# A transformer block on one Trainium2 core: where the users of one shared PSUM bank stand in the first token group

## The chip, the cores and the metric

The kernel runs on one core of one Trainium2 chip. The metric is device time in microseconds (us), lower is better. A core has TensorE for matrix products (PE in the profile, PEld its weight loads), VectorE (DVE), ScalarE (ACT), GpSimd (POOL) and SyncE (SP, which here issues the transfers). The engines run side by side and wait for each other only through semaphores.

## The reference: what is computed

```python
xn = _layernorm(x, axis=-1)                    # x: 2 x 2048 tokens of 1024 channels
s = _L0_attn_ref(xn)                           # autocorrelation of a token, best 6 lags, softmax, shifted sum
g = _silu(_L0_ffn_ref(xn, w1q, a1, b1, w3q, a3, b3, w2q, a2, b2))
x = x + s * g
...
def _qlora_linear(x, wq, A, B):
    w = jnp.tile(wq, (1, 4))
    return x @ w.T + (x @ A.T @ B.T) * 0.5
gate = jax.nn.silu(_qlora_linear(x, w1q, a1, b1))      # hidden size 2752, rank 2
up = _qlora_linear(x, w3q, a3, b3)
return _qlora_linear(gate * up, w2q, a2, b2)
```

Since a weight is tiled four times, the four quarters of a token are summed first and multiplied by one quarter of the weight. If lag zero of the autocorrelation beats all others by a wide margin, the softmax gives it all the weight and `s` is `xn`; the kernel shows that margin with a small transform and keeps a general path for tokens where it fails.

## The kernel before: groups, chunks and the bank mb

The 4096 tokens are 8 groups of 512 (`i` from 0 to 7), a group 4 tiles of 128 (`q`). The hidden size is walked in 22 chunks, called pairs in the code (`p` from 0 to 21). For a pair TensorE forms the gate product in a bank `g` and the up product in a bank `u` (`up`, lines 1305 to 1327), six matmuls each, since every float32 operand is split in a high and a low fp16 part. The rank-2 terms come from `lora` (L1300), which runs ahead of each odd pair and serves that pair and the even one before it. ScalarE applies silu (`gate`), VectorE multiplies (`product`, writes `h`), and `z2` (L1412) and the down products follow. A bank `g`/`u` of pair p is free again when `product` of pair p-3 is done.

The order on every engine is written out by hand: small tables (`X_AT`, `C_AT`, `I_AT`, `HIGH_AT`, `LOW_AT`, `NORM_AT` and so on) say after which pair each piece of side work stands. Engines run their lists in order, so an instruction that waits holds all that is behind it on its engine.

In group 0 the kernel has side work that later groups don't have. It prepares the weights: a bound of each block's size (`w_bound`, squares with a sum, output `w_sq`), the power-of-two scale (`w_scale`), the high part on ScalarE (`w_high`, outputs `w_h`, `wp_h`) and the low part on VectorE (`w_low`, outputs `w_l`, `wp_l`). It forms the rank-4 projection of its own tokens (`z0`, `z0_spread`), split in three bf16 parts: `z_part[0]` and `z_part[1]` on ScalarE, `z_rest` and the last part with `zst` on VectorE. And it transposes the tokens of group 1 on TensorE (`second_x`, L1370, eight half tiles, each copied out by ScalarE to `xT`).

One PSUM bank, `mb`, is shared by all of this in turn: the eight half tiles of `second_x`, two `odd_power` products (L1337, each squared by ScalarE in `square`, output `sq`), the product `lags` (L1347), reduced by VectorE in `lag_gap` (L834, output `gp`, semaphore `gap_done`), and the one-column `flag_sum`. A user may write only when the one before it has been read.

GpSimd makes the quarter sums of the next group's tokens, `sums(i + 1, q)`: outputs `yh`, `xq`, `dd`, each a tensor_tensor on SBUF, as soon as ScalarE's `normalise` has written `xn` for that tile.

The waits in `second_x` before the change, with half tiles numbered `n` from 0 to 7:

```python
if n == 2:
    pe.wait_ge(wall_read, 3)
elif n == 4:
    pe.wait_ge(sq_done, 2)
elif n == 6:
    pe.wait_ge(gap_done, 1)
```

Of the kernel before, what the change touches and what calls it, by code (L numbers as in the profile page):

```python
# [16 lines left out]
NG = TOK // G  # L17
# [77 lines left out]
def build(nc, d):  # L95
# [3 lines left out]
    with ExitStack() as ctx:  # L99
# [9 lines left out]
        def sem(name):  # L109
            return ctx.enter_context(nc.semaphore(name))  # L110
# [95 lines left out]
        def block_cols(b):  # L206
            return pair_col(BLOCK[b]), HID if b == NB - 1 else pair_col(BLOCK[b + 1])
# [61 lines left out]
        x1_ready, x1_done = sem("x1_ready"), sem("x1_done")  # L269
# [15 lines left out]
        c_ready, sq_done, i_ready, gap_done = sem("c_ready"), sem("sq_done"), sem("i_ready"), sem("gap_done")  # L285
# [22 lines left out]
        STATS_AT = [(3, 7, 10, 14)] + [(1, 7, 13, 19)] * (NG - 1)  # L308
        NORM_AT = [(5, 10, 13, 17)] + [(2, 8, 14, 20)] * (NG - 1)
        Z_AT = [{}] + [{3 + 6 * q + r: (q, r) for q in range(3) for r in range(4)}] * (NG - 1)  # L310
        X_AT = {3: (0, 0), 4: (0, 1), 6: (1, 0), 7: (1, 1), 12: (2, 0), 13: (2, 1), 16: (3, 0), 17: (3, 1)}
        W2L_AT = {16: 0, 18: 1}
        C_AT = [(9, 11)] + [(5, 9)] * (NG - 1)
        I_AT = [(14,)] + [(11,)] * (NG - 1)
        FAR_AT = [(8, 12, 16, 20)] + [(4, 10, 16)] * (NG - 1)
        FAR0_AT = (5, 6, 7, 9)
        FLAG_AT = [18] + [18] * (NG - 1)
# [228 lines left out]
        def _(act):  # L546
            def A(out, in_, f=ACT.Identity, **kw):
                return nc.scalar.activation(out, in_, f, **kw)  # L548
# [25 lines left out]
            def gate(i, p):  # L574
                n = pair_rows(p)
                act.wait_ge(g_ready, at_pair(i, p))
                if p >= 2:
                    act.wait_ge(mult_done, at_pair(i, p - 2))
                A(sil[0:n, p % 2, :], gb[p % 3][0:n, :], ACT.Silu, scale=winv[0:n, 3 * block_of(p):3 * block_of(p) + 1]).then_inc(sil_done, 1)
# [30 lines left out]
            def second_x(n):  # L610
                q, half = n // 2, n % 2
                act.wait_ge(x1_ready, n + 1)
                A(xT1[:, 4 * half:4 * half + 4, q * P:(q + 1) * P],
                  mb[:].rearrange("p (k t) -> p k t", k=4), ACT.Copy).then_inc(x1_done, 1)
# [23 lines left out]
            def w_bound(b, m):  # L638
                lo, hi = block_cols(b)
                act.wait_ge(w_loaded[b][m], 16)  # L640
                if b or m:
                    act.wait_ge(wsum_done, 2 * b + m)
                with nc.allow_low_precision(reason="a bound with a margin"):
                    A(w_sq[:, :, 0:hi - lo], raw_w[b][:, m], ACT.Square,
                      accum_out=wsum[:, 2 * b + m:2 * b + m + 1]).then_inc(wsum_done, 1)

            def w_high(b, m, k=0):
                lo, hi = block_cols(b)
                s = wscl[:, 3 * b + m:3 * b + m + 1]
                act.wait_ge(wscl_done, min(b, 2) + 1)  # L650
                if b == 0:
                    A(wt_h[m][:, k, lo:hi], raw_w[b][:, m, k, :], scale=s).then_inc(wh_done, 1)
                    return
                if b == NB - 1:
                    A(wp_h[:, :, 64 * m:64 * m + 64], raw_w[b][:, m, :, hi - lo - 64:hi - lo], scale=s)
                A(wt_h[m][:, :, lo:min(hi, LAST * P)], raw_w[b][:, m, :, 0:min(hi, LAST * P) - lo],
                  scale=s).then_inc(wh_done, 1)
# [9 lines left out]
            def b_scale(b):  # L667
                lo, hi = BLOCK[b] // 2, BLOCK[b + 1] // 2
                act.wait_ge(b_rest_done, 2 if b < 2 else 4)
                act.wait_ge(wscl_done, min(b, 2) + 1)  # L670
                s = wscl[:, 3 * b + 2:3 * b + 3]
                if b == NB - 1:
                    hi = LAST // 2
                    A(bst[0:64, hi, :], bst[0:64, hi, :], ACT.Copy, scale=s[0:64])
                    A(bst[64:96, hi, 0:64], bst[64:96, hi, 0:64], ACT.Copy, scale=s[64:96])
                    A(bst[64:96, hi, 64:P], bst[64:96, hi, 64:P], ACT.Copy, scale=half_u[64:96, 0:1])
                A(bst[:, lo:hi, :], bst[:, lo:hi, :], ACT.Copy, scale=s).then_inc(b_done, 1)
# [45 lines left out]
            A(rsb[:], mb[:], ACT.Copy).then_inc(rsb_done, 1)  # L723
            w_high(0, 1, 1)
            w_bound(1, 0)
            act.wait_ge(z0_ready, 2)
            A(z_part[0][:], mb[:], ACT.Copy).then_inc(z0_part, 1)
            w_bound(1, 1)
            act.wait_ge(z0_rest, 1)
            A(z_part[1][:], z_rest[:], ACT.Copy).then_inc(z0_part, 1)  # L730
            b_scale(0)
            for i in range(NG):
                last = i + 1 == NG
                for p in range(NP_):
                    gate(i, p)
                    if i == 0:
                        if p in X_AT:
                            second_x(2 * X_AT[p][0] + X_AT[p][1])
                        for b, m in HIGH_AT.get(p, ()):
                            w_high(b, m)  # L740
                        if p in B_AT:
                            b_scale(B_AT[p])
                        for b, m in BOUND_AT.get(p, ()):
                            w_bound(b, m)
                        if p in CAST_AT:
                            b_cast(CAST_AT[p])
                        if p in W2_AT:
                            w2_high(W2_AT[p])
                    if p in C_AT[i]:
                        square(i, C_AT[i].index(p))  # L750
                    if i == 0 and p in FAR0_AT:
                        far_lags(0, FAR0_AT.index(p))
                    if not last and p in NORM_AT[i]:
                        normalise(i + 1, NORM_AT[i].index(p))
                    if not last and p in FAR_AT[i]:
                        far_lags(i + 1, FAR_AT[i].index(p))
                    if p % 4 == 1 and p > 1:
                        folded_high(i, p // 4 - 1)
                    if i == 0 and p == LAST:
                        b2_high()  # L760
                tail_shifts(i)
                folded_high(i, HN)
                if i and not last:
                    far_lags(i + 1, 3)
                z2_copies(i)
                if i == 0:
                    second_z()
                for q in range(4):
                    if i and not last and q == 3:
                        z_copy(i + 1)  # L770
                    down(i, q)
                    if i == 0 and q:
                        first_mean(q - 1)
                if i == 0:
                    first_mean(3)
# [3 lines left out]
        def _(dve):  # L779
# [379 lines left out]
            for i in range(NG):  # L1159
# [4 lines left out]
                for p in range(NP_):  # L1164
                    if i == 0 and p - 1 in I_AT[0]:
                        lag_gap(0)
# [14 lines left out]
                    if i == 0 and p == 4:  # L1181
                        w_scale(2, 2, mb[:, 0:6])
                    if i and p - 1 in I_AT[i]:
                        lag_gap(i)
# [49 lines left out]
        def _(pe):  # L1234
# [103 lines left out]
                o.then_inc(c_ready, 1)  # L1338

            def lags(i):  # L1340
                if i == 0:
                    pe.wait_ge(x1_done, 6)
                pe.wait_ge(sq_done, at_group(i, 2, 2))
                for q in range(4):
                    t = slice(q * P, (q + 1) * P)
                    for c in range(2):
                        o = mm(mb[:, t], sq[:, c, t], inv[:, 0, :], start=c == 0, stop=c == 1)  # L1347
                o.then_inc(i_ready, 1)
# [5 lines left out]
            def second_x(q, half):  # L1354
                n = 2 * q + half
                buf, loaded, count = front_buf(1, q)
                pe.wait_ge(loaded, count)
                if n == 0:
                    pe.wait_ge(z0_rest, 1)
                else:  # L1360
                    pe.wait_ge(x1_done, n)
                if n == 2:
                    pe.wait_ge(wall_read, 3)
                elif n == 4:
                    pe.wait_ge(sq_done, 2)
                elif n == 6:
                    pe.wait_ge(gap_done, 1)
                for k in range(4):
                    c = P * (4 * half + k)
                    o = nc.tensor.transpose(mb[:, k * P:(k + 1) * P], buf[:, c:c + P], ident[:])  # L1370
                o.then_inc(x1_ready, 1)
# [177 lines left out]
            for i in range(NG):  # L1549
# [3 lines left out]
                for p in range(NP_):  # L1553
# [3 lines left out]
                    if i == 0 and p == 5:  # L1557
                        pe.wait_ge(x1_done, 2)
                        scale_sum(2, mb, 0)
                        scale_sum(3, mb, 3)  # L1560
                    if i == 0 and p in X_AT:
                        second_x(*X_AT[p])
                    if p in C_AT[i]:
                        odd_power(i, C_AT[i].index(p))
                    if p in I_AT[i]:
                        lags(i)
# [83 lines left out]
```

## Time and profile before

| | |
|---|---|
| time, median of 3 runs | 848.99 us (848.12 to 849.02) |
| the profiled execution | 848.62 us, its span 846.8 us |
| PE busy | 830.9 us, 98% of the span |
| DVE / ACT / POOL busy | 577.6 / 331.2 / 148.0 us (68 / 39 / 17%) |

The span is the stretch between the first and the last instruction that the profiler records; the 1.8 us around it belong to the execution's own time. A line of the timeline gives the start, the duration, the engine, the source line, the operation, what it writes and reads, and in brackets the idle time of the engine before it with the instruction that ended it. Durations of neighbours overlap a little, since instructions are pipelined; the pitch from one start to the next is the time that an instruction takes of its engine. All times of the timeline are from the span's start. Matmul ends are modelled.

### The profile page before, as it was taken

The page shows a single profiled execution, that of the slowest core. Times are in us where ns is not written, and L with a number is a line of the kernel's source. Part 1 is how long each engine was busy: PE and PEld are TensorE (multiplying, and loading weights), DVE is VectorE, ACT ScalarE, POOL GpSimd, SP SyncE. Part 2 cuts the span into 40 slices and gives each one's busy share as a digit, 9 for nine tenths or more (in the row PEclk, how much of TensorE's full clock was granted, in tenths as well). Part 3 has the DMA queues.
Part 4 walks back from the last instruction along what each step waited for, and adds up shares of the span by engine and source line. Part 5 has one row for each costly group of instructions (what it writes and reads, how often), then busy time and mean ns, then how long its engine had stood idle before and what let it go on. Part 6 is the DMA issues. An engine that isn't in the chain of part 4 may idle for free.

```text
span 846.8 us, 11242 instructions
## 1 busy us (share of the span) xinstructions
PE 830.9 (98%) x4200; PEld 441.2 (52%) x4200; DVE 577.6 (68%) x941; ACT 331.2 (39%) x544; POOL 148.0 (17%) x240
## 2 busy tenths in 40 slices
PE   6998999999999999999999999999999999999997
PEld 4443575335744367334763347534575336844366
DVE  7888744686776876688667776678766686744535
ACT  5886645434133342333423333333323434122231
POOL 5224101222012220122201221023201222000000
PEclk9999999999999999999999999999999999999999
DMA  9721026000230003300042000501015000220004
GB/s 285 269 89 50 26 107 218 26 26 26 82 142 26 26 26 125 100 26 26 26 151 74 26 26 26 199 28 48 26 49 176 26 1 0 101 100 1 1 2 149
DMA packets 18903, 62.13 MB, mean 73 GB/s; under 512 B 2464, under 2 KB 4224, under 8 KB 18576
## 3 DMA queue, kind: packets, MB, share of 16 engines
q1 hardware_dynamic: 18832, 61.28, 21.1%
q8 instruction: 33, 0.54, 0.3%
q14 instruction: 38, 0.31, 0.1%
HBM read 44.49 MB, written 16.78 MB: 72 GB/s over the span
## 4 chain that ended last, share of the span: by engine, by line
PE 87%; DVE 5%; ACT 3%; issue 2%; DVEq 2%; DMA 1%; SPq 0%; POOL 0%; ACTq 0%; POOLq 0%
PE g L1249 25%; PE u L1249 23%; PE zb L1412 5%; PE g L1471 4%; PE u L1471 4%; PE u L1480 4%; PE g L1480 4%; PE u L1478 4%; PE g L1478 4%; PE g L1300 3%; PE mb L1337 1%; DMA xf<-in_x 1%; DVEq L868 1%; PE g L1474 1%; PE u L1474 1%
## 5 line engine op out<-in xcount | busy, mean ns | idle before, releaser
L548 ACT ACTIVATE sil<-g,winv 128x512 f32<-128x512 f32 (+1 forms) x176 | 119.8, 683 | 267.1 <-PE g L1300 239.2
L852 DVE SCALAR_TENSOR_TENSOR h<-u,winv,sil 128x512 f32<-128x512 f32 x168 | 125.6, 749 | 122.6 <-ACT sil L548 107.1
L1249 PE MATMUL g<-xt,w_h 128*128 128x512 f16 x656 | 196.2, 381 | 0.0
L1249 PE MATMUL u<-xt,w_h 128*128 128x512 f16 x656 | 195.1, 379 | 0.0
L809 DVE CUSTOM_DVE_ANT_0 junk<-xn,abc 128x1024 bf16<-128x1024 f32 x96 | 120.3, 1253 | 6.0 <-issue 2.7
L1249 PE MATMUL u<-xt,w_l 128*128 128x512 f16 x328 | 124.3, 379 | 0.0
L1249 PE MATMUL g<-xt,w_l 128*128 128x512 f16 x328 | 124.3, 379 | 0.0
L1249 PEld LDWEIGHTS u<-xt,w_h 128*128 128x128 f16 x656 | 64.2, 98 | 77.4
L1249 PEld LDWEIGHTS g<-xt,w_h 128*128 128x128 f16 x656 | 55.6, 98 | 83.3 <-issue 31.6
L449 POOL TENSOR_TENSOR ve<-mv,three 128x1 f32<-128x1 f32 x30 | 6.5, 218 | 471.9 <-DVE mv L791 471.8
L548 ACT ACTIVATE gg<-g 128x512 f32<-128x512 f32 x32 | 19.1, 598 | 139.8 <-PE g L1474 64.1
L1003 DVE SCALAR_TENSOR_TENSOR ob<-xr,c_mean,gg 128x1024 f32<-128x1024 f32 x27 | 34.6, 1283 | 55.6 <-ACT gg L548 34.4
L1471 PE MATMUL g<-w_h,hf_h 128*128 128x512 f32 x174 | 71.8, 413 | 0.3 <-ACT gg L548 0.3
L1471 PE MATMUL u<-w_h,hf_h 128*128 128x512 f32 x174 | 69.0, 396 | 0.0
L1480 PE MATMUL u<-w_h,hf_l 128*128 128x512 f32 x145 | 57.5, 397 | 0.0
L1480 PE MATMUL g<-w_h,hf_l 128*128 128x512 f32 x145 | 57.4, 396 | 0.0
L1478 PE MATMUL u<-w_l,hf_h 128*128 128x512 f32 x145 | 57.4, 396 | 0.0
L1478 PE MATMUL g<-w_l,hf_h 128*128 128x512 f32 x145 | 57.4, 396 | 0.0
L864 DVE TENSOR_TENSOR acc<-acc,h 128x512 f32<-128x512 f32 x80 | 56.8, 710 | 0.0
L1249 PEld LDWEIGHTS g<-xt,w_l 128*128 128x128 f16 x328 | 32.1, 98 | 38.7
L1249 PEld LDWEIGHTS u<-xt,w_l 128*128 128x128 f16 x328 | 32.1, 98 | 38.7
L1412 PE MATMUL zb<-h,a2st 128*6 128x512 f32 x352 | 48.5, 593 | 0.0
(255 smaller groups left out, 1131.2 us busy)
## 6 DMA issues: line engine op xcount, KB each, us to landing
xr<-in_x SPq DMA_DIRECT2D x32, 512.0 KB, 4.6
out_x<-ob SPq DMA_DIRECT2D x31, 512.0 KB, 2.9
xf<-in_x SPq DMA_DIRECT2D x30, 512.0 KB, 3.3
raw_w<-in_w2t SPq DMA_DIRECT2D x1, 2560.0 KB
abc<-in_a SPq DMA_DIRECT2D x1, 2048.0 KB, 8.2
raw_w<-in_w1t SPq DMA_DIRECT2D x2, 768.0 KB, 8.5
raw_w<-in_w3t SPq DMA_DIRECT2D x2, 768.0 KB, 9.8
raw_w<-in_w1t SPq DMA_DIRECT2D x1, 704.0 KB, 12.8
```

The lines of the kernel that those rows point to most:

```text
L548: return nc.scalar.activation(out, in_, f, **kw)
L809: nc.vector.tensor_tensor_reduce(junk[:], xn[:], abc[:, r, :], 1.0, 0.0, ALU.mult, ALU.add, zt[:, q, r:r + 1]).then_inc(z_done, 1)
L852: stt(out=h[0:n, p % NH, :], in0=up, scalar=winv[0:n, 3 * block_of(p) + 1:3 * block_of(p) + 2], in1=sil[0:n, p % 2, :], op0=ALU.mult, op1= ...
L864: o = tt(acc[0:rows, b, :], a, h[0:rows, p % NH, :], ALU.add)
L1003: stt(out=o[:], in0=x[:], scalar=c_mean[:, q:q + 1], in1=gg[:], op0=ALU.subtract, op1=ALU.mult)
L1249: o = mm(bank[:], a, x, start=opens and t == 0, stop=closes and t == len(terms) - 1)
L1300: o = mm((gb, ub)[s % 2][k % 3][:], bst[32 * s:32 * s + 32, p // 2, :], zst[32 * s:32 * s + 32, :], start=s >= 2 and not first, stop=s < 2 ...
L1412: o = mm(zb[c:c + 6, :], a2st[:, p, :], h[:, p % NH, :], start=n == 0, stop=p + 4 >= NP_)
L1471: mm(bank[:], hf_h[:, n, t], w2_h[:, n, c:c + 512], start=n == 0, stop=False)
L1474: mm(bank[:], hf_l[:, n, t], w2_l[:, n, c:c + 512], start=False, stop=True).then_inc(dn_ready, 1)
L1478: mm(bank[:], hf_h[:, n, t], w2_l[:, n, c:c + 512], start=False, stop=False)
L1480: mm(bank[:], hf_l[:, n, t], w2_h[:, n, c:c + 512], start=False, stop=False)
```

## The change

Five edits, all in group 0 or ahead of it.

1. `X_AT`: the third tile of `second_x` (half tiles 4 and 5) moves from after pairs 12 and 13 to after pairs 14 and 15. The fourth stays after 16 and 17.
2. `I_AT[0]`: `lags` moves from after pair 14 to after pair 13, and with it `lag_gap` on VectorE, from ahead of `product(15)` to ahead of `product(14)`.
3. Waits on TensorE follow: half tile 4 now waits for `gap_done` instead of the squares, half tile 6 for no reader but ScalarE's copy of half tile 5, and `lags` no longer waits for half tile 5's copy.
4. On ScalarE in group 0 `square` stands ahead of `w_high`, `b_scale` and the other weight work of the same pair.
5. Ahead of group 0 `w_bound(1, 1)` stands before `z_part[0]` instead of behind it.

```diff
-        X_AT = {3: (0, 0), 4: (0, 1), 6: (1, 0), 7: (1, 1), 12: (2, 0), 13: (2, 1), 16: (3, 0), 17: (3, 1)}
+        X_AT = {3: (0, 0), 4: (0, 1), 6: (1, 0), 7: (1, 1), 14: (2, 0), 15: (2, 1), 16: (3, 0), 17: (3, 1)}
...
-        I_AT = [(14,)] + [(11,)] * (NG - 1)
+        I_AT = [(13,)] + [(11,)] * (NG - 1)
@@ -723,9 +723,9 @@
             w_bound(1, 0)
+            w_bound(1, 1)
             act.wait_ge(z0_ready, 2)
             A(z_part[0][:], mb[:], ACT.Copy).then_inc(z0_part, 1)
-            w_bound(1, 1)
             act.wait_ge(z0_rest, 1)
@@ -736,6 +736,8 @@
                         if p in X_AT:
                             second_x(2 * X_AT[p][0] + X_AT[p][1])
+                        if p in C_AT[0]:
+                            square(0, C_AT[0].index(p))
                         for b, m in HIGH_AT.get(p, ()):
                             w_high(b, m)
@@ -746,7 +748,7 @@
-                    if p in C_AT[i]:
+                    if i and p in C_AT[i]:
                         square(i, C_AT[i].index(p))
@@ -1338,8 +1340,6 @@
             def lags(i):
-                if i == 0:
-                    pe.wait_ge(x1_done, 6)
                 pe.wait_ge(sq_done, at_group(i, 2, 2))
@@ -1362,8 +1362,6 @@
                 if n == 2:
                     pe.wait_ge(wall_read, 3)
                 elif n == 4:
-                    pe.wait_ge(sq_done, 2)
-                elif n == 6:
                     pe.wait_ge(gap_done, 1)
```

TensorE's instructions before, from the end of pair 12 on (L1370 is `second_x`, L1300 `lora`, L1412 `z2`, L1347 `lags`, L1249 a pair's products):

```order
L1370 MATMUL mb<-ident,xf_65 128x128 [waits sq_done,x1_done,x0_loaded]
...
L1412 MATMUL zb<-h,a2st 6x512 [waits mult_done]
L1412 MATMUL zb<-h,a2st 6x512 x3
L1370 MATMUL mb<-ident,xf_65 128x128 [waits x1_done,x0_loaded]
...
L1347 MATMUL mb<-inv,sq 128x128 [waits sq_done,x1_done]
L1347 MATMUL mb<-inv,sq 128x128 x7
L1300 MATMUL g<-zst,bst 128x512 [waits mult_done]
```

And now, over the same pairs (line numbers of the changed file; L1368 is `second_x`, L1302 `lora`, L1410 `z2`, L1251 a pair's products):

```order
L1410 MATMUL zb<-h,a2st 6x512 [waits mult_done]
L1410 MATMUL zb<-h,a2st 6x512 x3
L1347 MATMUL mb<-inv,sq 128x128 [waits sq_done]
L1347 MATMUL mb<-inv,sq 128x128 x7
...
L1368 MATMUL mb<-ident,xf_65 128x128 [waits gap_done,x1_done,x0_loaded]
L1368 MATMUL mb<-ident,xf_65 128x128 x3
L1302 MATMUL g<-zst,bst 128x512 [waits mult_done]
```

The transposes after pairs 12 and 13 are gone, `lags` follows `z2` of pair 13 at once, and the first transposes after it, at the end of pair 14, carry the wait for VectorE's reduction.

VectorE's instructions before, from `w_low` of pair 12 on (L1081 and L1085 are `w_low`, L852 `product`, here of pairs 13 and 14, L864 `add_chunk`, L788 to L791 `stats`, L887 `folded_low`, L834 `lag_gap`):

```order
L1081 SCALAR_TENSOR_TENSOR wp_l<-raw_w_134,wscl,wp_h 128x64 [waits wh_done]
L1085 SCALAR_TENSOR_TENSOR w_l<-raw_w_134,wscl,w_h 128x640
L852 SCALAR_TENSOR_TENSOR h<-u,winv,sil 128x512 [waits u_ready,z2_done,sil_done] x2
L864 TENSOR_TENSOR acc<-h 128x512 [waits hfl_done,mult_done]
L788 BN_STATS bn<-xf_66 128x6 [waits stats_done,x1_loaded]
L789 BN_STATS bn<-xf_66 128x6
L791 BN_AGGR mv<-bn 128x2
L887 TENSOR_TENSOR hf_l<-acc,hf_h 128x512 [waits hfh_done]
L834 TENSOR_REDUCE gp<-mb 128x4 [waits i_ready]
```

And now (L1083 and L1087 are `w_low`, L854 `product`, L836 the reduction):

```order
L1083 SCALAR_TENSOR_TENSOR wp_l<-raw_w_134,wscl,wp_h 128x64 [waits wh_done]
L1087 SCALAR_TENSOR_TENSOR w_l<-raw_w_134,wscl,w_h 128x640
L854 SCALAR_TENSOR_TENSOR h<-u,winv,sil 128x512 [waits u_ready,z2_done,sil_done]
L836 TENSOR_REDUCE gp<-mb 128x4 [waits i_ready]
```

The reduction stands right behind `product(13)`, five instructions earlier than before, but still behind all of `w_low` of pair 12.

ScalarE's instructions before, from `gate(12)` on (sil is `gate`, xT `second_x`, dd,far `far_lags`, bst `b_scale`, w_h from raw_w_137 `w2_high`, xn `normalise`, here of group 1's third tile):

```order
L548 ACTIVATE sil<-g,winv 128x512 [waits mult_done,g_ready]
L548 ACTIVATE xT_147<-mb 128x4x128 [waits x1_ready]
L548 ACTIVATE dd,far<-dd 128x256 [waits diff_done]
L548 ACTIVATE sil<-g,winv 128x512 [waits mult_done,g_ready]
L548 ACTIVATE xT_147<-mb 128x4x128 [waits x1_ready]
L548 ACTIVATE bst<-bst,wscl 64x128 [waits wscl_done,b_rest_done]
...
L548 ACTIVATE w_h<-raw_w_137 128x1024 [waits wl_done,w2_loaded]
L548 ACTIVATE xn<-xf_65,nm,rs 128x1024 [waits diff_done,sum_done,dev_done]
```

And now:

```order
L548 ACTIVATE sil<-g,winv 128x512 [waits mult_done,g_ready]
L548 ACTIVATE dd,far<-dd 128x256 [waits diff_done]
L548 ACTIVATE sil<-g,winv 128x512 [waits mult_done,g_ready]
L548 ACTIVATE bst<-bst,wscl 64x128 [waits wscl_done,b_rest_done]
...
L548 ACTIVATE w_h<-raw_w_137 128x1024 [waits wl_done,w2_loaded]
L548 ACTIVATE xn<-xf_65,nm,rs 128x1024 [waits diff_done,sum_done,dev_done]
```

Two copies of transposes have left, so nothing between `gate(12)` and this `normalise` waits for a transpose any more.

## Rows read from the trace of the kernel before

**Rows 1.** Who TensorE waited for in the whole span: total us, times, longest

```profile
PE g L1300 <- DVE zst L1156: 0.6, 1, 0.6
...
PE g L1471 <- ACT gg L548: 0.3, 1, 0.3
```

**Rows 2.** Timeline of TensorE, end of pair 12 to the start of pair 17

```profile
65.70 0.63 PE L1370 MATMUL mb<-ident,xf 128*128 128x128 f32 x4 [1.09 <-ACT sq L548]
...
69.28 1.04 PE L1412 MATMUL zb<-h,a2st 128*6 128x512 f32 x8
70.25 0.66 PE L1370 MATMUL mb<-ident,xf 128*128 128x128 f32 x4
70.75 0.59 PE L1249 MATMUL g<-xt,w_h 128*128 128x512 f16 x2
...
73.34 0.61 PE L1347 MATMUL mb<-inv,sq 128*128 128x128 f16 x8
73.88 0.39 PE L1300 MATMUL g<-zst,bst 32*128 32x512 bf16 x1
...
76.81 0.59 PE L1259 MATMUL g<-xt,w_h 128*128 128x512 f16 x2
...
80.73 0.63 PE L1370 MATMUL mb<-ident,xf 128*128 128x128 f32 x4 [1.17 <-DVE gp L834]
81.29 0.39 PE L1300 MATMUL g<-zst,bst 32*128 32x512 bf16 x1
```

**Rows 3.** Timeline of ScalarE around the z parts

```profile
24.46 0.60 ACT L548 ACTIVATE z_part<-mb 128x512 bf16<-128x512 f32 x1 [1.45 <-PE mb L1525]
24.96 1.47 ACT L548 ACTIVATE w_sq<-raw_w 128x1536 bf16<-128x1536 f32 x1
...
26.42 0.62 ACT L548 ACTIVATE z_part<-z_rest 128x512 bf16<-128x512 f32 x1
```

**Rows 4.** Timeline of VectorE around the z parts

```profile
25.76 0.88 DVE L1092 SCALAR_TENSOR_TENSOR bst<-b_part,low,raw_b 128x640 bf16<-128x640 bf16 x1
27.07 0.75 DVE L1156 SCALAR_TENSOR_TENSOR zst<-z_part,low,z_rest 128x512 bf16<-128x512 bf16 x1 [0.43 <-ACT z_part L548]
```

**Rows 5.** Transfers issued between 12.1 and 12.93 us: KB, us to landing

```profile
raw_w<-in_w3t SPq DMA_DIRECT2D x1, 768.0 KB, 8.7
```

**Rows 6.** Timeline of VectorE, w_low of pair 12 and the reduction

```profile
70.99 0.28 DVE L1081 SCALAR_TENSOR_TENSOR wp_l<-raw_w,wscl,wp_h 128x64 f16<-128x64 f32 x1
...
71.98 0.74 DVE L852 SCALAR_TENSOR_TENSOR h<-u,winv,sil 128x512 f32<-128x512 f32 x1
...
79.91 0.68 DVE L834 TENSOR_REDUCE gp<-mb 128x4 f32<-128x512 f32 x1
```

**Rows 7.** Timeline of ScalarE, gate(11) to normalise of the third tile

```profile
62.86 0.67 ACT L548 ACTIVATE sil<-g,winv 128x512 f32<-128x512 f32 x1
...
64.97 0.58 ACT L548 ACTIVATE sq<-mb 128x512 f16<-128x512 f32 x1
...
71.44 0.74 ACT L548 ACTIVATE bst<-bst,wscl 64x128 bf16<-64x128 bf16 x2
...
73.79 1.23 ACT L548 ACTIVATE xn<-xf,nm,rs 128x1024 f32<-128x1024 f32 x1
```

**Rows 8.** Timeline of GpSimd: yh of that tile, and xq in group 1

```profile
75.10 1.27 POOL L496 TENSOR_TENSOR yh<-xn 128x512 f32<-128x512 f32 x1 [7.22 <-ACT xn L548]
...
204.04 1.11 POOL L498 TENSOR_TENSOR xq<-yh 128x256 f32<-128x256 f32 x1
```

**Rows 9.** Timeline of VectorE around that xq

```profile
203.87 0.68 DVE L887 TENSOR_TENSOR hf_l<-acc,hf_h 128x512 fp32r<-128x512 f32 x1
204.47 1.22 DVE L873 TENSOR_TENSOR half_a<-half_a,h 64x512 f32<-64x512 f32 x1
```

**Rows 10.** Stretches: length, PE busy, granted clock (1.00 is 2.4 GHz), DMA share, GB/s

```profile
14.60:18.00 3.40, 1.28 (x9) 1.00 1.10 276
18.00:21.50 3.50, 3.45 (x22) 0.52 1.03 401
```

## The prediction

> **What bounds the kernel now.** I read the page first: TensorE is busy for 98% of the span, so only time in which it stands still, or runs at a lower clock, can be won or lost. Then who TensorE waited for: in the whole span it waited 0.6 us for `zst` ahead of the first LoRA product and 0.3 us for `gg`, its only wait after group 0 [rows 1]. The other two waits that concern the change stand in its timeline: 1.09 us for the square of the second odd power at 65.70, and 1.17 us for the reduction of `lag_gap` at 80.73 [rows 2]. Both are waits for the bank `mb`. These three, 1.09 + 1.17 + 0.6 = 2.9 us, are all that the change can take away; it adds and removes no work. The profiled execution took 848.62 us, 0.37 below the median of 848.99 us; the sums are differences from it and are put on the median at the end.
>
> **Edit 5, `w_bound(1, 1)` ahead of `z_part[0]`.** ScalarE stands idle for 1.45 us, from 23.01 to 24.46, until TensorE has written `mb` [rows 3]. `w_bound(1, 1)` takes 26.42 - 24.96 = 1.46 us. It must wait for the sum of the bound before it, which I put at 0.1 us, so it ends at about 24.55 and `z_part[0]` comes 0.1 us late. Its weights were issued by 12.9 us and took 8.7 us [rows 5], so they lie there by 21.6. Behind it the row is free: `z_rest` then ends 0.1 us later than now, at about 25.9, since `b_step` follows it at 25.76 [rows 4]; `z_part[1]` needs 0.62 us and is done at 26.6 instead of 27.04; `b_step` is done at about 26.7, and so `zst` starts at 26.7 instead of 27.07. That is 0.4 us off the wait of 0.6 us. What stands behind `zst` (the scale of block 1, the high parts, pairs 2 to 4) hangs on it through VectorE and ScalarE, so I carry the 0.4 us through. **Term: -0.4 us.**
>
> **Edits 1 to 4 on TensorE**, in the times of the trace, the 0.4 us left out. Without the transposes at 65.70 and their wait, LoRA of pair 13 starts at 65.70 - 1.09 = 64.6. A pair with LoRA takes 76.81 - 73.88 = 2.93, `z2` 0.97, `lags` 73.88 - 73.34 = 0.54, pair 14 takes 73.34 - 70.75 = 2.59 [rows 2]. So pair 14 ends at 64.6 + 2.93 + 0.1 + 0.97 + 0.54 + 2.59 = 71.7, and there `second_x(2, 0)` wants the bank. It now waits for VectorE's reduction of the product that `lags` wrote at 69.
>
> VectorE can't give it by then. Its queue in these pairs is full: `w_low` of pair 12 runs up to 71.98, then comes `product(13)`, 0.74 us [rows 6]; the reduction is next, at 72.7. From its start to TensorE's first transpose it takes 80.73 - 79.91 = 0.82 us [rows 2, 6]. So the transposes start at 73.5 at the earliest: the two waits have become one of 1.8 us, in another place. From there: transposes to LoRA 81.29 - 80.73 = 0.56, pair 15 2.93, half tile 5 0.50, pair 16 2.59, half tile 6 0.56. ScalarE's copies of half tiles 4 and 5 lie beside pairs of 2.6 us and need 0.6. LoRA of pair 17 comes at 73.5 + 7.14 = 80.64 instead of 81.29. **Term: -0.65 us**, if VectorE runs as in the trace.
>
> **What ScalarE's new order does to VectorE.** `normalise` of the third tile stood at 73.79. Now nothing ahead of it waits for a transpose. `w_high(3, 1)` and the square together end where they did, at 64.97 + 0.49 = 65.5, in either order; two silus of 0.6 us each (0.67 us long, overlapping) and a `far_lags` of about half a us bring ScalarE to 67.1, and from `b_scale(3)` to `normalise` it is 73.79 - 71.44 = 2.35 [rows 7]. So `normalise` starts at 69.5, and GpSimd's `yh` follows by 75.10 - 73.79 = 1.31, at 70.8 instead of 75.1 [rows 7, 8]. That is in the middle of `w_low` of pair 12.
>
> The trace shows what these two do to each other. In group 1 `xq` on GpSimd starts at 204.04 during a `folded_low` of VectorE that ends at 204.55; `xq` then takes 1.11 us, and VectorE's next instruction, started at 204.47, takes 1.22 us for an operation of 0.68 [rows 8, 9]. So the one that came first keeps on, and the two take turns. Applied to pair 12: `yh` starts at 70.8, gets its turn when the present `w_l` ends at 71.0, and holds till 72.3; the small `wp_l` of 70.99 follows till 72.5; then either the last `w_l` (to 73.3) or first `xq`, 0.6 us, and then `w_l` (to 73.9). `product(13)` starts at 73.1 to 73.8 instead of 71.98: **+1.1 to +1.8 us** on the reduction and on TensorE, whose one wait is now 3.0 to 3.6 us. I take the middle, **+1.45 us**; the bounds are 0, if VectorE keeps its turn or ScalarE comes 1.2 us later, and 2.5, if `yh` (1.27 us) and both short operations behind it (`xq` and `dd`; `xq` without its own wait is 1.11 - 0.51 = 0.6 us) fall on it. Where VectorE's list runs late, `product(14)` is next, but it waits for its silu, which comes with LoRA of pair 15 behind the same transposes.
>
> The Trainium skill ("SBUF — State Buffer", section "Who interferes with whom") has this as a rule: a VectorE instruction with two SBUF inputs and a GpSimd instruction that reads SBUF take one shared pair of ports, the first for its whole length, and the other fully blocks; by it the sum is the one just made, and without it the change would bring the two first terms alone. The trace agrees, with 1.22 us against 0.68 in rows 9, and this rule speaks against the change.
>
> Edit 4 at pair 9 costs nothing: `b_scale(2)` goes behind the square, and its LoRA is a pair away. The later load into the buffer of tile 2 (after half tile 5, now 77 us) serves group 2.
>
> **The sum:** -0.4 - 0.65 + 1.45 = +0.4 us, 849.0 us for the profiled execution and **849.4 us** on the median. Its own range is +0.05 to +0.75 by the two orders of turns, with some tenths for the prologue: 848.7 to 850.2.
>
> **The rivals.** *The clock falls in the long wait (slower).* In the stretch from 14.60 to 18.00 TensorE was busy for 1.28 of 3.40 us, and in the next 3.5 us its granted clock was 0.52, that is 1.2 GHz, then full again [rows 10]. The wait of 3.0 to 3.6 us is one piece with no work, though with dense work on both sides, and the waits of 1.1 us now leave the clock up. If it falls as there, it costs 3.5 x (1 - 0.52) = 1.7 us: 851.1 us with the sum above. With -1.05 us from the two terms it is slower by over 0.2% once the collision takes more than 1.05 us. The skill ("TensorE: Matmul & The Clock Gate", Part 1) says that the gate passes half of the pulses once the engine has been idle, and lets all pass once it has been busy; by it both outcomes are open here, as by the rows.
>
> *No collision.* `normalise` comes after 71 us, or VectorE goes first: the reduction is at 72.7 and the change gives 0.4 + 0.65 = 1.05 us, 847.9 us. For it: ScalarE's place is a sum of eight steps. Against it: it would have to be off by 1.2 us.
>
> *The waits simply go*, as if the reduction were done by 71.7: 2.3 + 0.4 = 2.7 us, 846.3 us. Against it stands VectorE's full queue: the reduction would have to come 1.8 us earlier, and nothing in the change takes work off VectorE.
>
> **How the numbers follow.** What a measurement of this kernel can tell from no change is 0.2%, 1.7 us. The forecast has 0.50, the clock 0.27, no collision 0.14, the waits gone 0.04, others 0.05. Faster by over 0.2%: the waits gone and a share of the others, 0.05. Slower: most of the clock's part (with the low end of the collision it stays within 1.7 us) and some others, 0.26. The same: 0.69. The range goes from no collision, 847.9, to the clock with the long collision, 848.99 + 0.75 + 1.7 = 851.4.
>
> **What would show it.** Each step has its place in the changed profile: `zst` starts by 26.7; TensorE's list of waits has no square and a single wait for `gp` at half tile 4, of 1.8 us without and 3 or more with the collision; `yh` of the third tile starts near 70.4 and `w_l` of pair 12 or the `wp_l` ahead of it is longer than 0.88 or 0.28; the granted clock in the 4 us behind that wait is 1.00 or about 0.5. The prediction is wrong if the wait for `gp` is under 1 us, if another wait comes up behind pair 17, where VectorE and ScalarE now have idle time, or if the 0.4 us are lost between pairs 1 and 12.

## The result, and the profile after

| | before | after |
|---|---|---|
| median of 22 runs each | 848.65 us (847.68 to 849.99) | 850.04 us (848.33 to 851.39) |
| ratio to before, 95% interval | | 1.0014 [1.0008, 1.002] |
| profiled execution, its span | 848.62, 846.8 us | 851.11, 849.3 us |
| mean granted clock in it | 0.996 | 0.993 |

The change costs 1.4 us. At 0.14% that is inside the 0.2% called the same, and 850.04 us lies inside the range. But it is 0.6 us above the point of 849.4, the difference from before is more than three times the +0.4 of the sum, and how it came about is not what the sum says.

First, who TensorE waited for (total us, times, longest), the one wait that has grown by more than 0.1 us (the reduction had 1.2 us in before):

```profile
PE mb L1368 <- DVE gp L836: 2.7, 1, 2.7
```

The wait for the square is gone, as forecast, the wait for `zst` is gone too, where 0.2 us were to be left, and one wait for the reduction stands at half tile 4. The timeline of TensorE, to be read against [rows 2] (the first row is LoRA of pair 1, which stood at 27.88 before):

```profile
27.28 0.38 PE L1302 MATMUL g<-zst,bst 32*128 32x512 bf16 x1
...
66.96 1.04 PE L1410 MATMUL zb<-h,a2st 128*6 128x512 f32 x8
67.93 0.62 PE L1347 MATMUL mb<-inv,sq 128*128 128x128 f16 x8
...
73.87 1.09 PE L1368 MATMUL mb<-ident,xf 128*128 128x128 f32 x4 [2.72 <-DVE gp L836]
74.89 0.60 PE L1302 MATMUL g<-zst,bst 32*128 32x512 bf16 x1
...
80.30 0.60 PE L1368 MATMUL mb<-ident,xf 128*128 128x128 f32 x4
...
83.86 0.38 PE L1302 MATMUL g<-zst,bst 32*128 32x512 bf16 x1
```

The transposes behind the wait take 1.09 us instead of 0.63 and the LoRA product 0.60 instead of 0.39. That is the clock. The granted clock of these stretches shows it (start and end, length, PE busy, granted clock, DMA share, GB/s):

```profile
72.00:74.00 2.00, 0.13 (x1) 0.81 0.00 0
74.00:76.00 2.00, 2.00 (x10) 0.50 0.00 0
76.00:78.00 2.00, 2.00 (x7) 0.50 0.00 0
78.00:80.00 2.00, 2.00 (x6) 0.50 0.00 0
80.00:82.00 2.00, 2.00 (x12) 0.98 0.10 18
```

After a wait of 2.72 us TensorE works some 6 us at 1.2 GHz. Why the wait is that long stands in VectorE's and GpSimd's rows, against [rows 6] and [rows 8]:

```profile
70.38 1.29 DVE L1083 SCALAR_TENSOR_TENSOR wp_l<-raw_w,wscl,wp_h 128x64 f16<-128x64 f32 x1
71.59 0.87 DVE L1087 SCALAR_TENSOR_TENSOR w_l<-raw_w,wscl,w_h 128x640 f16<-128x640 f32 x1
72.39 0.74 DVE L854 SCALAR_TENSOR_TENSOR h<-u,winv,sil 128x512 f32<-128x512 f32 x1
73.05 0.67 DVE L836 TENSOR_REDUCE gp<-mb 128x4 f32<-128x512 f32 x1
```

```profile
70.19 1.39 POOL L496 TENSOR_TENSOR yh<-xn 128x512 f32<-128x512 f32 x1 [2.93 <-ACT xn L548]
71.66 1.39 POOL L498 TENSOR_TENSOR xq<-yh 128x256 f32<-128x256 f32 x1
```

`yh` now starts at 70.19, beside `w_low` of pair 12. The small `wp_l` takes 1.29 us instead of 0.28, since it stands behind `yh`; then `w_l` runs in its usual 0.87 and it is `xq` that stands behind it, with 1.39 us. So the engines took turns, VectorE lost one turn, 1.0 us, and `product(13)` and the reduction came that much late. This is the collision of the prediction in its shorter order. The prediction named a rule of the Trainium skill ("SBUF — State Buffer", section "Who interferes with whom"); these rows agree with it, with 1.29 us against 0.28.

**How the 2.5 us of these two spans add up.** From LoRA of pair 1 to LoRA of pair 17 it was 81.29 - 27.88 = 53.41 us and is 83.86 - 27.28 = 56.58: +3.17. The sum's own -0.65 is in it, the collision with 73.87 - 27.28 = 46.59 against 73.5 - 27.88 = 45.62, +0.97, and the clock with 83.86 - 73.87 = 9.99 against 7.14, +2.85. Together 3.17. LoRA of pair 1 itself came 0.60 us earlier, which leaves 2.57. Much of the clock's part is this execution's own: it is the longest in any profile here, and the median is higher than before by 1.4 us, not by 2.5.

### The profile page after: what moved, and what is told of

The parts are those of the page before. It is cut to its first block, busy times and chain, and to the rows that moved or that the text cites. A ratio compares the mean times of both kernels' runs of the same rounds, so it can differ in the third digit from the quotient of the medians.

```text
span 849.3 us, 11241 instructions
## 1 busy us (share of the span) xinstructions
PE 833.7 (98%) x4200; PEld 442.3 (52%) x4200; DVE 578.4 (68%) x941; ACT 331.4 (39%) x544; POOL 148.1 (17%) x240
## 4 chain that ended last, share of the span: by engine, by line
PE 88%; DVE 5%; ACT 2%; issue 2%; DVEq 1%; DMA 1%; SPq 0%; POOL 0%; ACTq 0%; POOLq 0%
PE g L1251 25%; PE u L1251 23%; PE zb L1410 5%; PE g L1469 4%; PE u L1469 4%; PE u L1478 4%; PE g L1478 4%; PE u L1476 4%; PE g L1476 4%; PE g L1302 3%; PE mb L1339 1%; DMA xf<-in_x 1%; PE g L1472 1%; PE u L1472 1%; DVE junk L811 1%
## 5 line engine op out<-in xcount | busy, mean ns | idle before, releaser
L854 DVE SCALAR_TENSOR_TENSOR h<-u,winv,sil 128x512 f32<-128x512 f32 x168 | 125.7, 749 | 124.9 <-ACT sil L548 108.7
L1251 PE MATMUL g<-xt,w_h 128*128 128x512 f16 x656 | 197.1, 382 | 0.0
L1251 PE MATMUL u<-xt,w_h 128*128 128x512 f16 x656 | 196.0, 380 | 0.0
L1251 PE MATMUL g<-xt,w_l 128*128 128x512 f16 x328 | 124.8, 381 | 0.0
L1251 PE MATMUL u<-xt,w_l 128*128 128x512 f16 x328 | 124.6, 380 | 0.0
L1251 PEld LDWEIGHTS u<-xt,w_h 128*128 128x128 f16 x656 | 64.4, 98 | 78.0 <-issue 1.1
L1251 PEld LDWEIGHTS g<-xt,w_h 128*128 128x128 f16 x656 | 55.6, 98 | 83.8 <-issue 32.3
L1251 PEld LDWEIGHTS g<-xt,w_l 128*128 128x128 f16 x328 | 32.2, 98 | 39.0 <-issue 0.6
L1251 PEld LDWEIGHTS u<-xt,w_l 128*128 128x128 f16 x328 | 32.2, 98 | 39.0 <-issue 0.6
L1410 PE MATMUL zb<-h,a2st 128*6 128x512 f32 x352 | 48.5, 593 | 0.0
```

The lines of the kernel that those rows point to most:

```text
L854: stt(out=h[0:n, p % NH, :], in0=up, scalar=winv[0:n, 3 * block_of(p) + 1:3 * block_of(p) + 2], in1=sil[0:n, p % 2, :], op0=ALU.mult, op1= ...
L1251: o = mm(bank[:], a, x, start=opens and t == 0, stop=closes and t == len(terms) - 1)
L1410: o = mm(zb[c:c + 6, :], a2st[:, p, :], h[:, p % NH, :], start=n == 0, stop=p + 4 >= NP_)
```

## The experiments

In what follows, before and after stand for the two kernels and e1 to e12 for the experiments. Each was timed against the kernel before on the same chip: runs e1 to e4 share one set (848.25 us, 30 runs), e5 to e8 a second (848.14, 26 runs), e9 to e12 a third (847.98, 18 runs). LoRA(n) is the first LoRA product of pair n. "Clock up" says of a run that its mean granted clock was 0.999 or 1.0; of a place in a profile it says that the stretches there show 1.00. Of the 74 runs of the kernel before 36 were, with set medians of 847.67 to 847.84 us; in the others, 848.56 to 848.98 us, it was lower. So the executions of that kernel with the lower clock, about every second one, are 0.8 to 1.2 us longer; in its profile the low clock is the stretch of [rows 10].

**e1, edit 5 alone.**

```diff
             w_bound(1, 0)
+            w_bound(1, 1)
             act.wait_ge(z0_ready, 2)
...
-            w_bound(1, 1)
```

> The kernel before with edit 5 alone (w_bound(1, 1) ahead of z_part[0]). My theory: the wait for zst ahead of the first LoRA product goes and 0.4 to 0.6 us are carried through, the two waits for mb stay at 1.1 and 1.2 us, and the time falls by 0.4 to 0.6 us (ratio 0.9993 to 0.9995). Rival: the gain is used up in the waits for mb, which grow by it, ratio 1.000.

Measured: 848.25 us, ratio 1.0003 [0.9994, 1.0011]. The wait for `zst` is gone from its profile, and the time is the same. The rival of the expectation isn't the reason: the two waits for `mb` are 1.09 and 1.17 us in this profile, as before.

**e2, the changed kernel with `normalise` of the third tile one pair later** (`NORM_AT[0]` = 5, 10, 14, 17), so that `yh` can't meet `w_low`.

```diff
-        NORM_AT = [(5, 10, 13, 17)] + [(2, 8, 14, 20)] * (NG - 1)
+        NORM_AT = [(5, 10, 14, 17)] + [(2, 8, 14, 20)] * (NG - 1)
```

> The changed kernel with the normalise of the third tile after pair 14 in place of 13, so that GpSimd's yh starts when w_low of pair 12 is done. My theory: wp_l of pair 12 takes 0.28 us again in place of 1.29, the wait for the reduction shrinks from 2.7 to some 1.7 us, the clock stays up behind it, and the time is 1.0 us under the changed kernel's runs without a fall, some 1 us under the kernel before (ratio 0.9985 to 0.9995). Rival (the turn of GpSimd is not what holds VectorE, or doesn't matter): the wait stays 2.7 us and the ratio is that of the changed kernel, 1.001 to 1.002.

Measured: 847.68 us, ratio 1.0001 [0.9992, 1.001]. VectorE's rows lose the long `wp_l`, and TensorE's wait falls by 1.0 us:

```profile
70.39 0.28 DVE L1083 SCALAR_TENSOR_TENSOR wp_l<-raw_w,wscl,wp_h 128x64 f16<-128x64 f32 x1
70.59 0.88 DVE L1087 SCALAR_TENSOR_TENSOR w_l<-raw_w,wscl,w_h 128x640 f16<-128x640 f32 x1
...
72.05 0.68 DVE L836 TENSOR_REDUCE gp<-mb 128x4 f32<-128x512 f32 x1
```

```profile
27.27 0.39 PE L1302 MATMUL g<-zst,bst 32*128 32x512 bf16 x1 [1.10 <-DVE zst L1158]
...
72.87 0.63 PE L1368 MATMUL mb<-ident,xf 128*128 128x128 f32 x4 [1.72 <-DVE gp L836]
...
81.61 0.39 PE L1302 MATMUL g<-zst,bst 32*128 32x512 bf16 x1
```

72.87 - 27.27 = 45.60, where the sum without the collision had 45.62. The collision and its size are as expected, the time is not: a ratio of 0.9985 to 0.9995 was expected with the clock up, and in this execution it fell, behind a wait of only 1.72 us:

```profile
72.00:74.00 2.00, 1.13 (x10) 1.00 0.00 0
74.00:76.00 2.00, 2.00 (x7) 0.52 0.00 0
76.00:78.00 2.00, 2.00 (x7) 0.62 0.00 0
78.00:80.00 2.00, 2.00 (x13) 1.00 0.21 37
```

The profiled execution took 848.69 us. Four of the 12 runs took that or more, up to 850.66 us, and the other eight 847.17 to 847.98, so how often the clock falls behind this shorter wait can't be read from one profile.

**e3, the changed kernel with `w_low` of the last weights behind pair 14**, so that VectorE's queue ahead of the reduction is shorter by that `w_low`, 70.38 - 69.39 = 1.0 us for each of its two halves where nothing collides.

```diff
-                  11: ((3, 0, 0), (3, 0, 1)), 12: ((3, 1, 0), (3, 1, 1))}
+                  11: ((3, 0, 0), (3, 0, 1)), 14: ((3, 1, 0), (3, 1, 1))}
```

> The changed kernel with w_low of pair 12 (the low parts of block 3's up weights) moved to pair 14, behind the reduction. My theory, that VectorE's queue alone sets the wait for the bank: the reduction starts 2.0 us or more earlier, the wait at half tile 4 is under 0.5 us, nothing new waits, since these weights are needed late in pair 16, and the time is 2.3 to 2.9 us under the kernel before (ratio 0.9966 to 0.9975). Rival: the wait moves on, to pair 16's low products or to pair 17's silu, and the ratio is 0.9985 or above.

Measured: 845.54 us, ratio 0.9969 [0.9957, 0.9981]. The reduction starts at 70.15, TensorE comes at 71.07 and waits for nothing (71.07 - 27.37 = 43.70 from LoRA(1), against 43.82 by the sum if the waits simply went), and the clock stays at 1.00:

```profile
27.37 0.39 PE L1302 MATMUL g<-zst,bst 32*128 32x512 bf16 x1 [1.10 <-DVE zst L1158]
...
71.07 0.60 PE L1368 MATMUL mb<-ident,xf 128*128 128x128 f32 x4
...
78.09 0.39 PE L1302 MATMUL g<-zst,bst 32*128 32x512 bf16 x1
```

With this side work out of the reduction's way the wait and the collision are gone, the profile shows no fall of the clock, and the loss is gone with them. The rival "the waits simply go" needs just that, and gave -2.7 us. How much of the 2.7 us the late `w_low` would give without edits 1 to 3 was not tried.

**e4, the changed kernel with 12 useless products in the wait** (bank 0 of the gate, rewritten before it is read again).

```diff
+                    if i == 0 and p == 14:
+                        pe.wait_ge(mult_done, at_pair(0, 12))
+                        for t in range(12):
+                            mm(gb[0][:], wt_h[0][:, 0, 0:P], xt[:, 0, :], start=True, stop=True)
```

> The changed kernel with 12 useless matmuls (2.6 us of work into pair 15's bank, overwritten afterwards) ahead of half tile 4, in the wait for the reduction. Theory that the clock falls for want of work there: the clock stays 1.00 behind it in every run, no run reaches 851 us, and the profiled run is 2.8 us under the changed kernel's 851.11. Rival, the clock's fall has another cause: it falls as before, and the added work costs up to 2.6 us on top where it isn't covered.

Measured: 848.83 us, ratio 1.0006 [0.9997, 1.0015]. In its profile the transposes come as late as in that of after, and the clock is 1.00 behind them:

```profile
71.71 2.75 PE L1562 MATMUL g<-xt,w_h 128*128 128x512 f16 x12
74.60 0.63 PE L1368 MATMUL mb<-ident,xf 128*128 128x128 f32 x4
```

Five of the 11 runs have the clock up (median 848.37), where of the 54 runs with the long wait empty and nothing added at the start (after, e2, e5, e6) none has. That the clock would stay up in every run, as expected, is not shown: in the other six it was lower somewhere. TensorE did more work, its transposes came no earlier (46.59 us after LoRA(1), as in the profile of after), and the ratio is 0.0008 lower than that of the change, some 0.7 us; the two intervals overlap, so it is the count of clocks that speaks for the clock's part, more than the time.

**e5, the changed kernel again, and e6, the changed kernel without edit 5**, on one chip.

```diff
-            w_bound(1, 1)
             act.wait_ge(z0_ready, 2)
             A(z_part[0][:], mb[:], ACT.Copy).then_inc(z0_part, 1)
+            w_bound(1, 1)
```

> The changed kernel once more, on one chip with the three others of this call. My theory: the clock falls behind its wait of 2.7 us in every run, so that no run shows a mean granted clock of 1.000, where the kernel before shows it in about a third of its runs; time 1.0 to 1.8 us above the kernel before (ratio 1.001 to 1.002). Rival: the fall is rare, several runs reach 1.000 and these are at or below the kernel before.

> The changed kernel without edit 5. By my prediction's term it is 0.4 us slower than the changed kernel; the wait for the reduction at half tile 4 is 2.7 us and its cause the same. Rival, that the earlier z parts buy nothing (the alone run of edit 5 gave 1.0003 with an interval down to 0.9994): the same time as the changed kernel within 0.2 us.

Measured: 850.31 us, 1.0019 [1.0009, 1.0029], and 850.42 us, 1.0022 [1.0013, 1.0031]. Edit 5 again makes no difference. No run has the clock up, as expected of e5, but not for the reason given there: both profiles show the same wait, and the clock stayed up behind it, having fallen at the start instead. Of e5:

```profile
74.58 0.63 PE L1368 MATMUL mb<-ident,xf 128*128 128x128 f32 x4 [2.73 <-DVE gp L836]
...
81.62 0.39 PE L1302 MATMUL g<-zst,bst 32*128 32x512 bf16 x1
```

```profile
18.00:20.00 2.00, 1.95 (x16) 0.54 1.04 398
20.00:22.00 2.00, 2.00 (x12) 0.60 1.03 406
72.00:74.00 2.00, 0.00 (x0) 1.00 0.00 0
74.00:76.00 2.00, 1.42 (x11) 1.00 0.00 0
```

One profile can't tell what the wait costs: the same wait has both outcomes.

**e7, edit 4 alone** (the square ahead of the weights on ScalarE).

```diff
                             second_x(2 * X_AT[p][0] + X_AT[p][1])
+                        if p in C_AT[0]:
+                            square(0, C_AT[0].index(p))
...
-                    if p in C_AT[i]:
+                    if i and p in C_AT[i]:
```

> The kernel before with edit 4 alone (the squares ahead of the weight work on ScalarE). The wait of 1.1 us for the square goes. Here the transposes after pair 12 stay, ScalarE and VectorE behind them start earlier by as much, and the reduction comes at 78.8 instead of 79.9: the wait for it stays at 1.2 to 1.4 us and the time falls by 1.1 us, ratio 0.9985 to 0.9990. Rival, that VectorE's full queue fixes the reduction at 79.9 in this order too: the wait for it grows to 2.3 us, the clock may fall behind it, ratio 1.000 or above.

Measured: 847.10 us, ratio 0.9987 [0.9978, 0.9996]. Of the two waits for the bank the one for the square is gone and the other unchanged:

```profile
78.60 0.63 PE L1372 MATMUL mb<-ident,xf 128*128 128x128 f32 x4 [1.18 <-DVE gp L836]
```

Edit 4 gains 1 us by itself. Edits 1 to 3 turn it into a loss: e6, which has edits 1 to 4, took 850.42 us against 847.10 on the same chip.

**e8, e3 without edit 5; e9 and e10, the two again, on one chip.** The diffs are those above.

> The kernel with w_low of pair 12 at pair 14, this time without edit 5. Theory: all that edits 1 to 4 bring once VectorE's queue is out of the way is the 2.3 us of the two waits for mb, so 2.0 to 2.5 us under the kernel before (ratio 0.9970 to 0.9976), and edit 5 adds 0.4 us to that in the other version (0.9969 measured). Rival: edit 5 brought more than 0.6 us of that version's gain, and this one is at 0.9978 or above.

> The third experiment once more (the changed kernel with the low part of the last pair of weights after pair 14), now beside the same kernel without edit 5, on one chip. If edit 5 is worth 0.4 us, as the prediction had it, this one is 0.4 us faster than the next: about 845.1 against 845.5. If it costs what the two profiles suggest wherever the clock stays up at the start (zst at 26.56 against 25.88), it is 0.3 to 0.6 us slower than the next. Against the kernel before: about -2.7 us, ratio 0.997.

> Edits 1 to 4 with the low part after pair 14, and w_bound(1, 1) behind z_part[0] as before. Theory that edit 5 is worth nothing or a little less than nothing: 0 to 0.6 us faster than the run beside it, with zst at about 25.9 in a profile whose clock stays up at the start. Prediction's own term: 0.4 us slower.

Measured: e8 844.88 us, 0.9962 [0.995, 0.9975]; e9 (with edit 5) 845.80, 0.9969 [0.9957, 0.9981]; e10 (without) 845.51, 0.9969 [0.9957, 0.998]. My expectation of e8, that it would be slower than e3, missed. That e9 would be 0.3 to 0.6 us slower than e10 where edit 5 costs something agrees with the 0.29 us measured, though the two intervals overlap; of the runs with the clock up, e9 has four (median 845.68) and e10 two (844.84). What edit 5 does is seen in the profiles of e3 and e8, both with the clock up at the start. ScalarE with edit 5, and VectorE's `zst` below:

```profile
23.01 1.48 ACT L548 ACTIVATE w_sq<-raw_w 128x1536 bf16<-128x1536 f32 x1
...
24.49 0.58 ACT L548 ACTIVATE z_part<-mb 128x512 bf16<-128x512 f32 x1
...
26.56 0.75 DVE L1158 SCALAR_TENSOR_TENSOR zst<-z_part,low,z_rest 128x512 bf16<-128x512 bf16 x1
```

And without it, in e8:

```profile
23.27 0.60 ACT L548 ACTIVATE z_part<-mb 128x512 bf16<-128x512 f32 x1 [0.52 <-PE mb L1523]
23.76 1.48 ACT L548 ACTIVATE w_sq<-raw_w 128x1536 bf16<-128x1536 f32 x1
...
25.88 0.75 DVE L1158 SCALAR_TENSOR_TENSOR zst<-z_part,low,z_rest 128x512 bf16<-128x512 bf16 x1 [0.44 <-ACT z_part L548]
```

With the clock up TensorE has written `mb` by 23.27, so `w_bound(1, 1)`, which holds ScalarE until 24.49, makes `z_part[0]` wait. From the start of the product that writes `mb` to LoRA(1), over all profiles:

| us from it to LoRA(1) | with edit 5 | without |
|---|---|---|
| clock up at the start | 4.98 or 4.99 (e2, e3, e4, e9, e12) | 4.48 (e7, e8, e11) |
| clock low at the start | 3.96 (after), 3.95 (e1), 4.16 (e5) | 4.47 (before), 4.48 (e6, e10) |

In the profiles edit 5 takes 0.3 to 0.5 us off this stretch where the clock fell and adds 0.5 where it did not; the wait for `zst` is then 1.10 us (e2, e3) and not 0.60 (e8). The 0.5 us stay: from that product to LoRA(13) it is 64.03 - 22.38 = 41.65 us in e3 and 63.38 - 22.23 = 41.15 in e11, which has no edit 5. The gain at the low clock doesn't show in the times: the seven runs of e1 with the lower clock have a median of 848.75 us, those of before beside them 848.56.

**e11, e8 with 18 useless products of 128 columns in the gap at the start, and e12, the changed kernel with them.**

```diff
-            pe.wait_ge(dev_done, 12)
             pe.wait_ge(wall_read, 1)
+            for t in range(18):
+                mm(mb[:, 0:P], ones_h[:], ones_h[:], start=True, stop=True)
+            pe.wait_ge(dev_done, 12)
```

> The kernel of the run before, and 18 useless products of 128 columns into mb in the gap ahead of the transposes of rs (15.2 to 16.3 us in the profile), which nothing reads. Theory that the clock falls at the start for want of work there: the mean granted clock is 0.999 or 1.0 in nearly all runs, and the median is 0.3 to 1 us below that of the run without them. Rival, the clock falls there for another reason: the share of runs with a clock under 0.999 stays, and so does the time. If the products delay the transposes, up to 0.5 us slower instead.

> The changed kernel with the same 18 products at the start, and its wait of 2.7 us at the third tile as it is. Theory that the start and the long wait each take the clock down, more often one than both: with the start filled the wait's share shows alone; some runs keep the clock at 0.999 or 1.0 (about 847.5 us), others fall behind the wait (about 850). Rival, that the long wait takes it down in every run and the start had no part: no run at 0.999 or above, median about 850. In the profile: clock 1.00 from 18 to 22 us.

Measured: e11 844.84 us, ratio 0.9959 [0.9945, 0.9972], with the clock up in all five runs. The same kernel without the products has it up in two of seven runs on this chip (e10) and in four of five on another (e8), and e8's median of 844.88 us is no higher, so the count speaks for the products and is too small to show it alone. The gap in front of the transposes of `rs` (1.16 us in the profile of before) is filled:

```profile
15.54 1.18 PE L1542 MATMUL mb<-ones_h 128*128 128x128 bf16 x18 [0.26 <-DVE wall L1067]
16.56 0.60 PE L1545 MATMUL mb<-ident,rs 128*128 128x128 f32 x4
```

e12: 849.92 us, 1.0014 [1.0005, 1.0023]. Three of its 11 runs have the clock up, median 848.23; the other eight have 850.04. One of these eight, 848.22 us at a clock of 0.998, has the time of the three; the other seven took 849.86 us or more. In its profile the clock is full at the start and falls behind the wait:

```profile
18.00:20.00 2.00, 1.95 (x21) 1.00 1.03 397
...
74.00:76.00 2.00, 1.91 (x9) 0.51 0.00 0
76.00:78.00 2.00, 2.00 (x7) 0.63 0.00 0
```

```profile
74.09 1.08 PE L1368 MATMUL mb<-ident,xf 128*128 128x128 f32 x4 [2.73 <-DVE gp L836]
...
82.69 0.39 PE L1302 MATMUL g<-zst,bst 32*128 32x512 bf16 x1
```

So the clock falls behind the wait with a full clock at the start too, here in 7 or 8 runs of 11.

## Why the prediction was right, and where its sum was not

**Edits 1 to 4 on TensorE, -0.65: right.** The reduction could not come before VectorE was through `w_low` of pair 12, and the two waits became one. Without the collision the transposes were to come 45.62 us after LoRA(1); e2 shows 45.60. From them to LoRA(17) the sum had 7.14 us; with the clock up it is 7.04 (81.62 - 74.58 in e5). Edits 1 to 4 and the collision together are +0.24 us in the profile of e6, whose clock stayed up there: 81.32 - 27.67 = 53.65 from LoRA(1) to LoRA(17), against 53.41 in before.

**The collision, +1.45: right in kind, 0.45 us too large.** `normalise` was forecast at 69.5, less the 0.4 of edit 5, and came at 68.88; `yh` at 70.4, and came at 70.19. I had taken the middle of two orders of turns, and it was the shorter: 46.59 instead of 45.60, +1.0 us, and a wait of 2.72 us where 3.0 to 3.6 were forecast. The same `wp_l` of 1.28 or 1.29 us stands in the profiles of after, e4, e5, e6 and e12, so the order is steady.

**Edit 5, -0.4: this step failed.** By e1 (1.0003) and by e5 against e6 (850.31 and 850.42) it is worth nothing that can be measured. The step took ScalarE's idle time of 1.45 us from an execution in which the clock had fallen at the start. `w_bound` hides in it only then. With the clock up that idle time is 0.52 us (e8), the edit costs 0.5 us in the profiles, and the kernel before has its clock up in 36 of 74 runs.

**The clock behind the wait: its chance was mis-sized, its price nearly right.** I gave it 0.27. With the start filled it fell in 7 or 8 of 11 runs (e12). Its price was put at 1.7 us. From the transposes to LoRA(17), less the 7.04 us with the clock up, it was 8.74 - 7.04 = 1.7 us (e2), 8.60 - 7.04 = 1.6 (e12) and 2.95 in the profile of after, and by the two medians of e12 850.04 - 848.23 = 1.8. I had reasoned from the two waits of 1.1 us that leave the clock up, and from dense work on both sides. Neither helped: 1.72 us of waiting was enough in e2.

**Put together.** With the clock up on both sides the change cost 848.23 - 847.84 = 0.4 us, on three runs of e12; the profile's parts, +0.5 - 0.65 + 1.0 = +0.85, are somewhat more, and the difference is not resolved. Most executions of e12 add the clock's 1.8 us to that. As an estimate from e12, with 8 falls in 11 runs, 0.4 + 0.73 x 1.8 = 1.7 us over the runs of before with their clock up; before's own median stands 0.1 to 0.6 us above those runs, and what the changed kernel loses at the start comes on top. Measured were 1.39 (after) and 2.17 (e5), and how they divide is not resolved. That the sum's +0.4 agrees with the 0.4 us of the runs with the clock up is luck: by the profiles edit 5 was +0.5 where -0.4 stood, and a collision taken 0.45 us too long hid half of that. The result lies above the point since the rival that I called less likely is common. As a difference, +1.4 us is outside the sum's own range of +0.05 to +0.75 and inside the whole range only through that rival. The median of 850.04 us lies below the 850.2 of the sum's own range only because the forecast stood on 848.99 us, three runs of before, where 22 runs have 848.65.

What decides whether the clock falls in a given execution stays open. At the start it fell in 6 of the 12 profiles without the fill, and behind the wait in after, e2 and e12, but not in e5 and e6. The two falls don't look independent. Where it stayed up at the start it fell behind the long wait (e2, e12); where it had fallen at the start it fell again once (after) and stayed up twice (e5, e6). And if each had its own chance, as in before at the start (38 of 74) and in e12 at the wait (7 or 8 of 11), by this estimate 7 to 10 of the 54 runs would show neither, and none does. So the share of e12 may not be that of the changed kernel. The Trainium skill ("TensorE: Matmul & The Clock Gate", Part 1) says that the same kernel shows different numbers of slow matmuls from run to run; the runs here agree, in the middle of a kernel too, with the same 2.73 us in e5 and e12 and both outcomes.

## What to carry to other kernels

When a consumer is moved behind a producer on a full queue, add up what stands ahead of the producer there: here the move paid only once 2.0 us of side work had been taken from in front of it (-2.7 us instead of +1.4). Two waits of 1.1 us joined into one of 1.7 to 2.7 us are not the same wait, since the long one can take TensorE's clock with it. And look at the clock of the stretch from which an idle time is read: an idle time that another engine's low clock made is gone in the executions in which the clock stays up.

## What was not expected of the hardware

Useless products may keep the clock up: with 18 of them in a gap of TensorE at the start it was up in 5 runs of 5 (e11) against 6 of 12 without (e8 and e10), and with 12 in the long wait in 5 of 11 (e4), where 54 runs with neither had none. With 18 at the start and the wait empty it was 3 of 11 (e12). That they shorten the time isn't shown by these few runs.

The time of a copy of 128 x 4 numbers on VectorE varies between executions. It stands ahead of `product(0)`; in before it takes 0.16 us, in e5 0.76, and LoRA(3) then waits for `h`. Of e5:

```profile
29.76 0.76 DVE L802 COPY c_mean<-mv 128x4 f32<-128x4 f32 x1
...
31.23 0.38 PE L1302 MATMUL g<-zst,bst 32*128 32x512 bf16 x1 [0.45 <-DVE h L854]
```

It was so in e5, e7, e8, e9 and e10, with and without edit 5. LoRA(3) comes 0.5 us later in these (3.54 us after LoRA(1) in e5, 3.02 in before), and 0.3 us of that are left at LoRA(13) (36.95 against 36.67 in e6). GpSimd was then at its `dd` operations, of 0.7 us each:

```profile
29.08 1.41 POOL L485 TENSOR_TENSOR dd<-xr 128x256 f32<-128x256 f32 x2
```

In all 14 profiles the copy starts 0.67 to 0.69 us after this pair of `dd`, that is about where the first of the two ends and the second begins. That would fit a copy that either gets in between the two or stands behind the second. That the `dd` are the cause was not tried.
